# One pipeline over seven blocks for the node stage and the next layer's table stage of a three-layer graph network, with centred features and roots in place of logarithms

## The reference, cut to what matters

```python
for l in range(L):                                   # L = 3
    h = _ln(x, n1g[l], n1b[l])
    q, kn, vn = h[dst] @ Wq + bq, h[src] @ Wkn + bkn, h[src] @ Wvn + bvn
    ke, ve = edge_attr @ Wke + bke, edge_attr @ Wve + bve
    ...                                              # softmax of q*(kn+ke) over the edges of each dst
    agg = segment_sum((vn + ve) * alpha, dst)
    gate = sigmoid(agg @ Wih + bih + h @ Whh + bhh)
    upd = agg + gate * (h @ Wself + bself - agg)
    x = x + upd @ Wout + bout
    h2 = _ln(x, n2g[l], n2b[l])
    x = x + relu(h2 @ mW1 + mb1) @ mW2 + mb2
x = layernorm(x_first + _ln(x, ng, nb))              # after the last layer
```

## Time and profile before

| what | value |
|---|---|
| median of three runs | 9160.3 us (9158.19 to 9160.95) |
| profiled execution, its own time | 9160.98 us |
| its span | 9159.2 us |
| busy: POOL, DVE, PE, ACT | 6365.8, 5799.7, 3667.0, 2862.4 us |
| granted clock of PE, mean of the span | 0.686 |

### The profile page before, as it was taken

How to read it: one execution, slowest core, us unless ns; L and a number is a source line. 1 busy time by engine, 2 the same in 40 slices (tenths; PEclk the granted TensorE clock), 3 DMA queues, 4 the chain that set the end, 5 groups by cost and what they waited for, 6 DMA issues and landing times.

```text
span 9159.2 us, 45368 instructions
## 1 busy us (share of the span) xinstructions
PE 3667.0 (40%) x9857; PEld 2190.5 (24%) x9857; DVE 5799.7 (63%) x6114; ACT 2862.4 (31%) x2181; POOL 6365.8 (70%) x6734
## 2 busy tenths in 40 slices
PE   2677777776323233223342232322242222223325
PEld 1333333333122122212121221222222122212212
DVE  1666666666366776676437667767744776677673
ACT  0566666666122222222222222222221222222223
POOL 6677777774577777777457777777736777777762
PEclk9988888888656566555666665665576656656557
DMA  3455555554433443444234334434314443444331
GB/s 52 161 192 180 186 179 174 175 184 148 132 131 131 139 149 131 139 140 141 64 108 148 132 132 141 147 131 139 125 49 138 139 149 131 137 141 141 131 110 48
DMA packets 405487, 1247.08 MB, mean 136 GB/s; under 512 B 196101, under 2 KB 253910, under 8 KB 360006
## 3 DMA queue, kind: packets, MB, share of 16 engines
q0 software_dynamic: 215104, 429.19, 17.4%
q1 hardware_dynamic: 169606, 468.24, 14.6%
q10 hardware_dynamic: 20736, 349.23, 9.5%
HBM read 808.34 MB, written 437.84 MB: 136 GB/s over the span
## 4 chain that ended last, share of the span: by engine, by line
POOL 52%; issue 20%; PE 17%; ACT 7%; DVE 2%; DMA 1%; DVEq 1%; ACTq 0%; POOLq 0%; SPq 0%
POOL G L546 49%; PE PS L696 7%; PE PS L689 6%; ACT S L910 4%; POOL qexp L599 1%; PE PS L777 1%; POOL QQ L588 1%; PE PS L781 1%; ACT hid L886 1%; PE PS L666 1%; POOL s2exp L565 1%; POOL S L552 1%; POOL G L588 1%; ACT S L851 0%; ACT L855 0%
## 5 line engine op out<-in xcount | busy, mean ns | idle before, releaser
L546 POOL DMA_INDIRECT G<-tabkv,srcI x4704 | 4438.4, 944 | 1433.6 <-issue 1433.6
L756 PE MATMUL PS<-Wkvp,EA 128*128 128x256 f32 x4704 | 1672.9, 531 | 4296.3 <-DVE PX L1438 4217.8
L756 PEld LDWEIGHTS PS<-Wkvp,EA 128*128 128x128 f32 x4704 | 1253.4, 274 | 4716.5 <-DVE PX L1438 4381.7
L546 POOL DMA_INDIRECT G<-tab,srcI x1568 | 1481.4, 945 | 571.9 <-issue 507.2
L959 ACT ACTIVATE QQ<-QQ 128x3584 f32<-128x3584 f32 x84 | 538.4, 6410 | 3313.5 <-DVE PX L1438 3063.1
L1435 DVE TENSOR_TENSOR PS<-PS,G 128x512 f32<-128x512 f32 x588 | 408.4, 695 | 1593.3 <-DMA G<-tabkv,srcI 1575.3
L973 ACT ACTIVATE S<-SX 128x4480 f32<-128x4480 f32 x81 | 663.7, 8194 | 1238.4 <-DVEq L1462 1238.4
L689 PE MATMUL PS<-xT,W1p 128*128 128x512 f32 x1568 | 768.5, 636 | 252.2 <-ACT xT L847 243.1
L1424 DVE TENSOR_TENSOR_SCAN QQ<-PS,QQ 128x456 f32<-128x456 f32 x672 | 679.4, 1082 | 207.9 <-ACT QQ L959 192.3
L1461 DVE TENSOR_TENSOR_SCAN SX<-PS,SX 128x456 f32<-128x456 f32 x756 | 763.2, 1082 | 12.2
L696 PE MATMUL PS<-hid,W2p 128*128 128x512 f32 x1568 | 710.9, 596 | 34.2 <-ACT hid L886 31.5
(11 more groups left out here) (311 smaller groups left out, 4090.8 us busy)
## 6 DMA issues: line engine op xcount, KB each, us to landing
st<-S ACTq DMA_DIRECT2D x81, 2240.0 KB, 7.8
EA<-eaT SPq DMA_DIRECT2D x84, 1792.0 KB, 7.8
QQ<-qexp SPq DMA_DIRECT2D x84, 1792.0 KB, 7.3
st<-S ACTq DMA_DIRECT2D x27, 3668.0 KB, 12.0
G<-tabkv,srcI POOLq DMA_INDIRECT x4704, 2.5
xe<-in_edge_attr SPq DMA_DIRECT2D x28, 1792.0 KB, 8.1
qexp<-zeros SPq DMA_DIRECT2D x28, 1792.0 KB, 12.6
eaT<-eaC ACTq DMA_DIRECT2D x28, 1792.0 KB
```

The lines of the kernel that those rows point to most:

```text
L546: nc.gpsimd.indirect_dma_start(out=G[:, u, t, :], out_offset=None, in_=tab[:, :], in_offset=IND(ap=srcI[:, u, t:t + 1], axis=0)).then_inc( ...
L756: last = mm(PS[:, b + j // 2, 2 * P * (j % 2):2 * P * (j % 2) + 2 * P], EA[:, u, 4 * s + j, :], Wkvp[:, :], start=True, stop=True)
```

## The change

1. **One pipeline.** `HALVES` and the step-by-step orders go. Each step of a block gets a depth (below), block k's steps are shifted by 8k, and each engine's list is sorted by that sum. Steps of up to four blocks alternate in each list, and the next layer's table stage (after the third layer: the tail) follows in the same pipeline.
2. **Centred features.** nX is centred once, in the first table stage, by a product with `Cmat` (identity less mean). DVE centres the columns of `Wout` and `mW2` and their biases in each layer (`centred_weights`), so that x stays centred. The mean products and the centring of x go; each variance product stays.
3. **Roots.** Ln and Exp become one Sqrt on ACT and one DVE reciprocal of the whole block, followed by the same multiply and scale.
4. **The product with `Whh`** is made for all seven blocks ahead of the first turned block, right after nH and nX are loaded, and stays in PSUM.
5. **Weights.** The 30 loads of the first layer's node weights and 4 of the tail move to the start of the program, ahead of SP's loop over the first tables. Those of the later layers follow the previous boundary's last table store.
6. **Stores.** `tabq`, `hTd` and `xTd` are stored block by block like `tabkv`. DVE and PE hand over the projections one 128-column tile at a time, in two banks of PSUM taken in turn.
7. **The third layer** is written out behind a loop over the first two.

```diff
+def in_turn(depth):
+    order = sorted((SKEW * k + d, k, step) for k in range(NB) for step, d in depth.items())
...
+        NODE_PE = {"turn": 1, "gate": 3, "self": 5, "out": 7, "spread2": 10, "hidden0": 12, "hidden1": 14, "hidden2": 16,
+                   "hidden3": 18, "fold": 20}
+        NODE_ACT = {"agg": 2, "gate": 4, "square2": 9, "root2": 10.5, "relu0": 13, "relu1": 15, "relu2": 17, "relu3": 19}
+        NODE_DVE = {"sums": 0, "mix": 6, "onto": 8, "norm": 11, "onto2": 21}
+        TABLE_PE = {"spread": 23, "project0": 25, "project1": 25.5, "project2": 26.5, "project3": 27.5}
+        TABLE_ACT = {"square": 22, "root": 23.5}
+        TABLE_DVE = {"h": 24, "project0": 26, "project1": 26.5, "project2": 27.5, "project3": 28.5}
+        LAST_PE = {"spread": 23, "y_centre": 25, "y_spread": 27, "y_turn": 29}
+        LAST_ACT = {"square": 22, "root": 23.5, "y_square": 26, "y_root": 27.5}
+        LAST_DVE = {"y": 24, "y_norm": 28, "y_copy": 30}
...
             edge_weights(0)
             table_weights(0)
+            node_weights(0)
...
+            def store_tables1(m):
                 for k in range(NB):
-                    hold(sp, waits_sp, a_dve, l * A_DVE + 2 * NB + k + 1)
+                    hold(sp, waits_sp, projection_used, m * TILES + tiles_to(k))
...
+                    sp.dma_start(hTd[:, c0:c0 + w], nH[:, c0:c0 + w]).then_inc(h_out, 16)
+                    sp.dma_start(xTd[:, c0:c0 + w], nX[:, c0:c0 + w]).then_inc(h_out, 16)
...
-                edge_weights(l + 1)
-                hold(sp, waits_sp, b_dve, (l + 1) * (B_DVE * NB) + 1)
+                else:
+                    edge_weights(l + 1)
+                    store_tables1(l + 1)
+                    node_weights(l + 1)
...
-                    f(nB4[:, c0:c0 + w], PS[:, k, 0:w], ACT.Ln, bias=epsc[:, 0:1]).then_inc(ln_ready, 1)
...
-                    f(nB4[:, c0:c0 + w], nB4[:, c0:c0 + w], ACT.Exp, scale=-0.5).then_inc(done, 1)
+                f(nB4[:, c0:c0 + w], PS[:, k, 0:w], ACT.Sqrt, bias=epsc[:, 0:1]).then_inc(rooted, 1)
...
+            def scaled_by_spread(k, dst, g_, b_):
+                v.reciprocal(nB4[:, cols], nB4[:, cols])
+                settle()
+                tt(nB5[:, cols], nX[:, cols], nB4[:, cols], ALU.mult)
+                settle()
+                return ts(dst[:, cols], nB5[:, cols], cb[:, g_:g_ + 1], cb[:, b_:b_ + 1], ALU.mult, ALU.add)
```

More of the change, by code:

```diff
@@ L41, with tiles_to @@
 NTW, NLW = 19, 30
-A_DVE = 3 * NB
-B_PE, B_ACT, B_DVE = 11, 8, 5
-HALVES = (range(0, 3), range(3, NB))
+TILES = NPR
+SKEW = 8
 PD_RP, PD_END = 6, 7
 BSELF, BIH, BHH, BOUT, MB2, N1G, N1B, N2G, N2B, NGC, NBC = range(11)
-def after(steps, step, k):
-    half = HALVES[0] if k in HALVES[0] else HALVES[1]
-    return steps * half.start + step * len(half) + k - half.start + 1
+def tiles_to(k):
+    return min(4 * k + 4, TILES)
+def in_turn(depth):
+    order = sorted((SKEW * k + d, k, step) for k in range(NB) for step, d in depth.items())
+    return [(k, step) for _, k, step in order if not (step.startswith("project") and int(step[-1]) * P >= BLK[k][1])]
 def build(nc, A, out):
@@ L498, in _ @@
                     features(u, u)
-                table_weights(l + 1)
+                if not last:
+                    table_weights(l + 1)
                 hold(sp, waits_sp, q_put, (l + 1) * (16 * NT))
@@ L747, in _, with edges1 @@
+            def edges1(l):
+                hold(pe, waits_pe, projection_used, (l + 1) * TILES)
                 with pe.Fori(0, NCH // 2) as i:
@@ L773, in product @@
[L773 to L805, removed]
-                    on(half, folded, b_act, A_, B_ACT, 7)
@@ L822, in _ @@
-            tail(means(nB3), c_act, 0)
-            tail(means(nB2), c_dve, NB)
-            tail(means(nB3), c_act, 2 * NB)
-            tail(back, c_dve, 3 * NB)
+                hold(pe, waits_pe, b_x, l * 32 + 32)
+                mm(PS[:, 7, 0:2], Cmat[:, :], cb[:, BOUT:MB2 + 1], start=True, stop=True).then_inc(bias_centred, 1)
+                for k in range(NB):
+                    c0, w = BLK[k]
+                    mm(PS[:, k, 0:w], Wn[:, 2, :], nH[:, c0:c0 + w], start=True, stop=False, skip_group_check=True)
@@ new lines, in _ @@
+            pe.wait_ge(a_x, 16)
+            hold(pe, waits_pe, l_t, 16 * NTW)
+            for k in range(NB):
+                c0, w = BLK[k]
+                mm(PS[:, k, 0:w], Cmat[:, :], nX[:, c0:c0 + w], start=True, stop=True).then_inc(x0_centred, 1)
+            for k, step in in_turn(TABLE_PE):
+                table(k, step, 0)
+            with pe.Fori(0, L - 1) as l:
+                edges1(l)
+                hold(pe, waits_pe, l_t, (l + 2) * (16 * NTW))
+                for k, step in in_turn({**NODE_PE, **TABLE_PE}):
+                    if step in NODE_PE:
+                        node(k, step, l)
+                    else:
+                        table(k, step, l + 1)
@@ L955, in query, with layer @@
+            for k in range(NB):
+                root(k, 0)
+            def layer(l):
                 def query(n):
@@ L1413, in _, with layer @@
+            biases(0)
+            for k, step in in_turn(TABLE_DVE):
+                table(k, step, 0)
+            def layer(l):
                 v.memset(gate8[:, :, 0:1], 0.0)
@@ L1492, in mix @@
-                def mix(k, c0, w):
-                    stt(nB4[:, c0:c0 + w], PS[:, k, 0:w], cb[:, BSELF:BSELF + 1], nB2[:, c0:c0 + w], ALU.add, ALU.subtract)
+                centred_weights(l)
+            with dve.Fori(0, L - 1) as l:
+                layer(l)
+                biases(l + 1)
+                for k, step in in_turn({**NODE_DVE, **TABLE_DVE}):
+                    if step in NODE_DVE:
+                        node(k, step, l)
+                    else:
+                        table(k, step, l + 1)
@@ L1495, in mix @@
+            layer(L - 1)
+            dve.wait_ge(c_x, 80)
+            for k, step in in_turn({**NODE_DVE, **LAST_DVE}):
+                c0, w = BLK[k]
+                cols = slice(c0, c0 + w)
+                if step in NODE_DVE:
+                    node(k, step, L - 1)
+                elif step == "y":
+                    dve.wait_ge(rooted, L * NB + k + 1)
+                    scaled_by_spread(k, nB5, NGC, NBC)
                     settle()
-                    tt(nB4[:, c0:c0 + w], nB4[:, c0:c0 + w], nB3[:, c0:c0 + w], ALU.mult)
+                    tt(nB5[:, cols], nB5[:, cols], nX1[:, cols], ALU.add).then_inc(h_ready, 1)
+                elif step == "y_norm":
+                    dve.wait_ge(y_rooted, k + 1)
+                    v.reciprocal(nB4[:, cols], nB4[:, cols])
```

432 lines of the change are left out of this document (249 added, 183 removed).

## The result

The changed kernel takes 9175.97 us (median of 20 runs, 9171.94 to 9180.04), the kernel before 9160.98 (20 runs, 9157.22 to 9163.46): a ratio of 1.0016, 95% interval 1.0010 to 1.0022. That is slower, by less than the 0.2% set as the smallest telling change; 9166 was forecast. The profiled execution has a span of 9174.8 us.

What follows compares the result with a forecast made beforehand. POOL's chain was taken as the bound, so the change could matter only at the start, first table stage, boundaries and tail: 5.5 + 7 - 2 x 10.3 + 13 = +4.9 on 9161.0, so 9166 us, range 9122 to 9215.

Steps and rivals of the forecast that it cites:

- start: Program start: 34 early loads on SP delay the last table store and POOL's first gather, +5.5 us (bounds +3 and +12).
- table: First table stage: blocks of 12.8 us at half clock give +9.5, full clock -6; taken as +7 us.
- boundaries: Two boundaries between layers: gathers start earlier, at 4703.8 for 4714.1, a gain of 10.3 us each.
- tail: After the third layer: three reciprocals a block, 216 us from first fetch to end for 203, so +13 us.
- Reciprocal, 3.35 us: DVE's whole-block reciprocal of 512 columns, priced from two small ones at 0.15 + 512 x 0.00627 = 3.35 us.
- the low bound, 0.69 us: Lowest price for the whole-block reciprocal on DVE: a plain pass over 512 columns, 0.69 us.
- Pace: Filled pipeline: DVE's 18.7 us of work and three waits, 3.9 us, give 22.6 us a block at full clock.
- Clock: PE idles under h and restarts at half clock, lengthening the period by 2.4 us to 25.0.
- Both rivals: PE never runs into its stride: 9209 us, 22%, half all through 3%; PE keeps full clock: 9127 us, 17%.
- Weights ahead of the index: Each boundary: 30 weight loads, 18.5 us, precede SP's index load; POOL idles over 10 us before its first gather.
- the weights do not delay POOL: Rival at each boundary: weights issue faster or index loads are not late; 15.5 us less each, 9135 us, 5%.
- Switching a table: ACT's table loads priced at 1.28 us; rival at twice that: +31 on the forecast, 9198 us, 5%.

Runs made afterwards that it cites:

- e5: Changed kernel without the reciprocal in both norms of the pipeline, so its numbers come out different: 9031.09 us, ratio to the kernel before 0.9860.
- e7: Changed kernel with next-layer index and feature loads ahead of weights, early weight loads moved later, four extra PE products before hidden projections: 9120.92 us, ratio to before 0.9960.
- e6: Kernel before with only its logarithm and exponential replaced by a square root on ACT and a DVE reciprocal: 9282.47 us, ratio 1.0135.
- e4: Changed kernel with Ln and Exp back in place of square root and reciprocal, on slower chips: 10820.12 us, ratio to before 0.9972.
- f4: Changed kernel with Ln and Exp back in place of square root and reciprocal, in another set on slower chips: 10848.91 us, ratio to before 0.9980.
- e1: Changed kernel with the next layer's first two chunks' index and feature loads ahead of node weights, on slower chips: 10835.28 us, ratio to before 0.9984.

## Why the prediction was nearly right

**The sum.** Every term had its sign, and all came out 1 to 6 us from the forecast: start +6.3 for +5.5, table +2.8 for +7, boundaries -6.8 and -4.6 for -10.3 each, tail +17.9 for +13. The errors are 19 us in all, of which 8 cancel: +15.6 us for +4.9.

**Reciprocal, 3.35 us.** Exact, from two small rows. It was the one unshown price on which most hung; with the low bound, 0.69 us, the time would lie some 30 us above e5's 9031 (an estimate: a fifth of the reciprocals' price back).

**Pace.** Right at both clocks: 22.5 and 24.9 in e7, for 22.6 and 25.0. Its reasons hold too: the waits of DVE are where they were put, and at full clock their sizes are near (0.83, 1.81 and 1.53 us in e7's first period for 0.65, 1.6 and 1.65). At half clock they are 6.0 us in the changed kernel's period and 6.9 in e7's. One statement fails: DVE did not become the fullest engine. PE was busy 17.9 us for DVE's 16.8, at a clock of 0.85. The forecast had 13.4 for PE at full clock and counted 12 products of 512 columns where the lists have 13 (gate, self, out, two spreads, four hidden, four folding). The 22.6 came from DVE's work with its waits, so this did not move it.

**The boundary's 4 to 6 missing us.** The forecast had the sums of blocks 1 to 6 at 4513 to 4626 at full clock; shifted by the 9.2 us by which the first fetch is later, the trace has 4511, 4530, 4551, 4582, 4607, 4632. The last projection is 197.9 us behind the first fetch for 196.6. The rest is in the line on SP: gather 25.0 us behind it for 22.8, as four stores, the weights, a gap of 1 us and the landing follow. The gap furthest off is 31.1 us between the sums of blocks 3 and 4, where 27 were walked. PE's timeline of the changed kernel has a product of L818 there that waits for DVE:

```profile
4574.82 1.27 PE L818 MATMUL PS<-Wqkv,G 128*128 128x384 f32 x2 [4.72 <-DVEq L1516]
```

Block 0 has only one bank of PSUM, so its fourth projection waits until DVE, which is in another block's norm, has taken the third. One block on, PE has no such wait, the folding products behind it take 2.74 us where they took 4.09, and the period is 25.0 us. That this makes up the 4 us was argued, not tried.

**Clock.** The half-clock restart was right, its price for a period exact. Both rivals fall by their own conditions: the granted clock is 0.82 to 0.86 in the periods of the changed kernel, not 1.00, and the last projection ends 197.9 us behind the first fetch, not beyond 207. With e7's 1.00 in one period only, nothing shows what full clock all through would give.

**First table stage.** PE did idle 5.7 us under each h and restarted slowly, but blocks were 11 to 12 us apart, not 12.8. The term was taken at +7 between +9.5 and -6, and was +2.8; that it lay between is a choice that came out, not a mechanism that was worked out.

**Tail.** 220.8 us for 216. Its three reciprocals a block are 55 us of it by e5: without them it would be 38 us shorter than before, not 18 longer.

**Weights ahead of the index.** Right: POOL idled 17.1 us (over 10 was the sign), and e7 takes this wait away. Rival "the weights do not delay POOL" falls.

**Switching a table.** The Trainium skill ("ScalarE: Activation LUTs", What ACT_TABLE_LOAD costs) had 2.66 us a switch. Table loads of ACT in the node blocks of the changed kernel, with ACT's idle time ahead of them:

```profile
L996 ACT ACT_TABLE_LOAD x21 | 26.9, 1283 | 0.4
L1018 ACT ACT_TABLE_LOAD x15 | 19.2, 1283 | 0.3
L1002 ACT ACT_TABLE_LOAD x6 | 7.7, 1283 | 0.1
```

That is 42, two a block as forecast, each 1.283 us with nothing ahead of it; the measurement decides, and the page's drain does not show. The rival by that rule, 31 us more on the forecast, falls.

**What the forecast did not say.** It said that the reciprocals and the weights take back what the pipeline saves, and put a cheap reciprocal at some 25 us more a boundary. It did not put a number on the reciprocals together, so nobody could see in it that they held 144 us (e5), nine times what the change moved. That the sum came out within 11 us of such terms is in part luck.

## What to carry to other kernels

Price a replaced operation at its full size and count how often it stands on the path per block (here two, three in the tail), before asking what a pipeline hides: it hides work that nothing in the chain waits for, and every step behind a norm waited for the reciprocal, although no engine was full. If a change bundles a re-ordering with a swap of operations, time the swap both ways: added alone to the old kernel (e6, 124 us lost) and taken alone out of the new one (e4 and f4, 6 to 24 us won back, on the slower chips). The two need not agree, and only the second tells what undoing it would give. And when small loads are moved on a queue, look for the next transfer behind them that someone waits for: moving the index ahead won 16 us a boundary on one chip, and on another lost it again at the first boundary, where q's load then stood behind 49 others.

## What the runs showed of the hardware

- DVE's reciprocal of fp32 is 3353 ns for 128x512 and about 950 for 128x128, against 692 for a product of two tensors of 512 columns: nearly five times as long.
- With indirect gathers under way, SP's small loads went out every 2.8 us where they otherwise took 0.64, on the chips where the kernel takes 10850 us; on the other chip this wasn't seen (4719.00, 4719.65, 4720.32 in the changed kernel, behind its first gather).
- Those chips run the same instructions at the same pace (in one edge stage DVE is busy 1366.0 us for 1367.3, ACT 466.6 for 466.4, POOL 1480.5 for 1480.8), but move less: 115 GB/s over the span against 136. The edge stage is 2256 us there, not 2007. DVE's idle time grows at the place where it waits for the gathers in the changed kernel's trace: 2184 us ahead of e1's L1581, against 1563 for its like. The trace of e1 doesn't name what it waits for ("remote"), so that it is the gathers is argued:

```profile
L1581 DVE TENSOR_TENSOR PS<-PS,G 128x512 f32<-128x512 f32 x588 | 407.6, 693 | 2184.3 <-remote 2184.3
```
```profile
L1572 DVE TENSOR_TENSOR PS<-PS,G 128x512 f32<-128x512 f32 x588 | 408.3, 694 | 1562.6 <-DMA G<-tabkv,srcI 1557.2 <-PE PS L833 5.4
```
- PE's clock can go either way after nearly the same pauses: idle stretches of 0.89 and 1.83 us left it at full clock in one period of e7, 1.32 and 1.83 us at half in the next.
